# Last feed-forward of an eight-part transformer kernel: up products of four tiles issued together on disjoint rows of TensorE, each into its own bank

## What is computed

```python
unperm = jnp.argsort(perm)
t = x.reshape(b * l, Dm)[:, perm].reshape(b * l, h, d)      # 1024 tokens, 16 heads, 32
t = jnp.einsum('bhd,hdm->bhm', t, up)                       # 32 -> 128 for each head
t = jax.nn.gelu(t, approximate=False)
t = jnp.einsum('bhm,hmd->bhd', t, down)                     # 128 -> 32 for each head
out = t.reshape(b * l, h * d)[:, unperm]
```

## Time and profile before

| | us |
|---|---|
| median of 3 runs | 1510.85 (1509.21 to 1513.04) |
| the profiled execution, its own time | 1513.07 |
| its span in the trace | 1511.1 |
| PE busy / DVE / ACT / POOL | 1366.1 / 966.1 / 595.7 / 529.4 |
| mean granted clock of PE, share of full speed | 0.951 |

### The profile page before, as it was taken

One profiled execution on the slowest core, in us unless ns is written; L12 is line 12 of the kernel. 1 busy time (PEld: TensorE's weight loads), 2 busy tenths in 40 slices (PEclk: granted clock), 3 DMA queues, 4 the chain that ended last, 5 costly groups with the idle time before them and its releaser, 6 DMA issues.

```text
span 1511.1 us, 20683 instructions
## 1 busy us (share of the span) xinstructions
PE 1366.1 (90%) x6966; PEld 1020.6 (68%) x6966; DVE 966.1 (64%) x2126; ACT 595.7 (39%) x1605; POOL 529.4 (35%) x531
## 2 busy tenths in 40 slices
PE   2888877888998999989999889999999999998798
PEld 1555544666677777667877677777777787776555
DVE  6999956587432688832222666777777777776633
ACT  2777762361222345432212224444344443443331
POOL 5001003532222444132211354454454544543163
PEclk9999976998997999989999999999999999999799
DMA  5211112312121000011110231111211111100001
GB/s 163 57 43 30 33 32 91 104 63 82 44 77 49 1 15 29 1 42 43 42 42 15 91 105 35 49 36 50 64 56 49 36 49 63 57 22 1 7 1 56
DMA packets 54251, 72.76 MB, mean 48 GB/s; under 512 B 6130, under 2 KB 24818, under 8 KB 54148
## 3 DMA queue, kind: packets, MB, share of 16 engines
q1 hardware_dynamic: 53168, 70.20, 14.8%
q10 hardware_dynamic: 980, 1.25, 0.2%
HBM read 56.75 MB, written 10.49 MB: 44 GB/s over the span
## 4 chain that ended last, share of the span: by engine, by line
PE 65%; DVE 18%; issue 6%; POOL 5%; ACT 3%; DMA 2%; SPq 1%; POOLq 0%; DVEq 0%; ACTq 0%
PE bank L412 16%; PE bank L417 14%; PE bank L416 14%; PE bank L2318 3%; PE bank L2296 2%; PE bank L2211 2%; PE bank L2193 2%; DVE topv L1534 2%; DVE xn L1804 1%; DVE top L1528 1%; PE bank L2305 1%; PE bank L479 1%; DVE bank L1826 1%; DVE xn L1790 1%; DMA ring_l<-k 1%
## 5 line engine op out<-in xcount | busy, mean ns | idle before, releaser
L1005 POOL TENSOR_TENSOR ring_l<-stage,ring_h 128x512 fp32r<-128x512 f32 x133 | 179.0, 1364 | 236.4 <-ACT ring_h L1162 236.4
L412 PE MATMUL bank<-xTh_b,ring_h 128*128 128x512 f32 x464 | 191.0, 412 | 2.9 <-issue 1.5
L416 PE MATMUL bank<-xTl_b,ring_h 128*128 128x512 f32 x464 | 185.1, 399 | 0.0
L417 PE MATMUL bank<-xTh_b,ring_l 128*128 128x512 f32 x464 | 184.9, 399 | 0.0
L1113 POOL TENSOR_TENSOR q<-xn 128x512 f32<-128x512 f32 x64 | 82.3, 1285 | 221.0 <-DVE xn L1804 221.0
L412 PE MATMUL bank<-ring_h,o3h 128*128 128x512 f32 x256 | 125.5, 490 | 0.8 <-issue 0.8
L1444 ACT ACTIVATE probsT<-bank 128x512 f32<-128x512 f32 x64 | 38.3, 599 | 205.5 <-PE bank L2305 205.5
L1453 ACT ACTIVATE probs<-bank,nbias 128x128 f32<-128x128 f32 x256 | 90.7, 366 | 54.3 <-DVE nbias L1828 54.3
L412 PEld LDWEIGHTS bank<-xTh_b,ring_h 128*128 128x128 f32 x464 | 88.6, 191 | 23.3 <-issue 4.5
L417 PEld LDWEIGHTS bank<-xTh_b,ring_l 128*128 128x128 f32 x464 | 88.2, 190 | 21.7
L416 PEld LDWEIGHTS bank<-xTl_b,ring_h 128*128 128x128 f32 x464 | 88.7, 191 | 18.6
(11 more groups left out here) (323 smaller groups left out, 3324.9 us busy)
## 6 DMA issues: line engine op xcount, KB each, us to landing
stage<-in_units_dram SPq DMA_DIRECT2D x133, 256.0 KB, 3.1
ring_l<-k SPq DMA_DIRECT2D x64, 64.0 KB, 2.1
raw_k<-kvs SPq DMA_DIRECT2D x16, 256.0 KB, 2.1
raw_v<-kvs SPq DMA_DIRECT2D x16, 256.0 KB, 2.0
kraw<-raw_k SPq DMA_DIRECT2D x16, 256.0 KB, 3.4
v<-raw_v SPq DMA_DIRECT2D x16, 256.0 KB, 2.9
stage<-in_context_dram SPq DMA_DIRECT2D x8, 256.0 KB, 2.9
mask<-in_mask_row_dram SPq DMA_DIRECT2D x8, 256.0 KB, 3.1
```

The costliest lines, as they stand in the source:

```text
L412: ins = nc.tensor.matmul(out_ap, wh, mh, start=start, stop=False)
L416: nc.tensor.matmul(out_ap, wh, ml, start=False, stop=False)
L417: return nc.tensor.matmul(out_ap, wl, mh, start=False, stop=stop)
L1005: nc.gpsimd.tensor_tensor(ring_l[:, place_of(u), :], stage[:, u % STAGE, :], f32(ring_h[:, place_of(u), :]), ALU.subtract).then_inc(w_lo, 1)
```

## The change

The up products of a group's four heads are issued as one block of twelve matmuls (`four_up`): high by high of heads 0 to 3, then high by low of the four, then low by high. Each head has its own 32 rows of PE's array and its own bank, 0 to 3; the block raises `z_up` once, at its end. It waits for all four gelus of the group before. The permuted products move to banks 4 and 5, and from the third on each waits for the low half of the one two before. PE's new order is permuted(0), permuted(1), block 0, permuted(2), and then for each group o: down products 4o and 4o + 1, block o + 1, down products 4o + 2 and 4o + 3, permuted(o + 3). `tile_hi(o + 3)` and `tile_lo(o + 3)` now stand behind gelu and cast 4o + 3. `gel` has three places in place of two. `t2h` and `t2l` are laid over `tTh` and `tTl`, as permuted products still read `xTh_b` when the first sums of a group are copied away. The matmuls, gelus, casts and subtractions are the same in number and size.

```diff
--- before.py
+++ after.py
@@ -358,7 +358,7 @@
         e4.close()
         eB.close()
 
-        t2h, t2l = xTh_b, xTl_b
+        t2h, t2l = tTh, tTl
 
         kbh = xTh_b[:, 0:2, :].rearrange("r a (h j) -> r a h j", h=8)
         kbl = xTh_b[:, 2:4, :].rearrange("r a (h j) -> r a h j", h=8)
@@ -1150,7 +1150,7 @@
                 g.wait_ge(z_gh, n + 1)
                 if n >= 2:
                     g.wait_ge(z_dp, n - 1)
-                nc.gpsimd.tensor_tensor(gel_l[:, n % 2, :], gel[:, n % 2, :], f32(gel_h[:, n % 2, :]), ALU.subtract).then_inc(z_gl, 1)
+                nc.gpsimd.tensor_tensor(gel_l[:, n % 2, :], gel[:, n % 3, :], f32(gel_h[:, n % 2, :]), ALU.subtract).then_inc(z_gl, 1)
 
 
         @block.scalar
@@ -1468,7 +1468,7 @@
             def tile_hi(n):
                 a.wait_ge(z_t, n + 1)
                 c = slice(n % 2 * HALF, (n % 2 + 1) * HALF)
-                nc.scalar.activation(tTh[:, n // 2, c], bank[n % 4][:], ACT.Copy).then_inc(z_th, 1)
+                nc.scalar.activation(tTh[:, n // 2, c], bank[4 + n % 2][:], ACT.Copy).then_inc(z_th, 1)
 
             for n in range(3):
                 tile_hi(n)
@@ -1479,12 +1479,12 @@
                 nc.scalar.activation(t2h[:, o // 2, c], bank[6 + o % 2][:], ACT.Copy).then_inc(z_oh, 1)
 
             for n in range(32):
-                a.wait_ge(z_up, n + 1)
-                if n >= 2:
-                    a.wait_ge(z_gl, n - 1)
-                nc.scalar.activation(gel[:, n % 2, :], bank[4 + n % 2][:], ACT.Gelu).then_inc(z_g, 1)
-                if n < 5:
-                    tile_hi(n + 3)
+                a.wait_ge(z_up, n // 4 + 1)
+                if n >= 3:
+                    a.wait_ge(z_gl, n - 2)
+                nc.scalar.activation(gel[:, n % 3, :], bank[n % 4][:], ACT.Gelu).then_inc(z_g, 1)
+                if n % 4 == 3 and n // 4 + 3 < 8:
+                    tile_hi(n // 4 + 3)
                 if n % 4 == 2 and n > 4:
                     last_hi(n // 4 - 1)
             last_hi(7)
@@ -1852,7 +1852,7 @@
             def tile_lo(n):
                 v.wait_ge(z_th, n + 1)
                 c = slice(n % 2 * HALF, (n % 2 + 1) * HALF)
-                nc.vector.tensor_tensor(tTl[:, n // 2, c], bank[n % 4][:], f32(tTh[:, n // 2, c]), ALU.subtract).then_inc(z_tl, 1)
+                nc.vector.tensor_tensor(tTl[:, n // 2, c], bank[4 + n % 2][:], f32(tTh[:, n // 2, c]), ALU.subtract).then_inc(z_tl, 1)
 
             for n in range(3):
                 tile_lo(n)
@@ -1878,9 +1878,9 @@
                 v.wait_ge(z_g, n + 1)
                 if n >= 2:
                     v.wait_ge(z_dp, n - 1)
-                nc.vector.tensor_copy(gel_h[:, n % 2, :], gel[:, n % 2, :]).then_inc(z_gh, 1)
-                if n < 5:
-                    tile_lo(n + 3)
+                nc.vector.tensor_copy(gel_h[:, n % 2, :], gel[:, n % 3, :]).then_inc(z_gh, 1)
+                if n % 4 == 3 and n // 4 + 3 < 8:
+                    tile_lo(n // 4 + 3)
                 if n % 4 == 3 and n > 4:
                     last_lo(n // 4 - 1)
             last_lo(7)
@@ -2335,44 +2335,58 @@
             t.wait_ge(ln_lo, B * (LN_L3F[1] + 1))
             def permuted(n):
 
-                if n >= 4:
-                    t.wait_ge(z_tl, n - 3)
+                if n >= 2:
+                    t.wait_ge(z_tl, n - 1)
                 c = slice(n % 2 * HALF, (n % 2 + 1) * HALF)
                 for k in range(KT):
                     if n == 0:
                         t.wait_ge(z_pick, k + 1)
                     w = pick[:, k, n // 2 * P:(n // 2 + 1) * P]
-                    nc.tensor.matmul(bank[n % 4][:], w, xTh_b[:, k, c], start=k == 0, stop=False)
-                    ins = nc.tensor.matmul(bank[n % 4][:], w, xTl_b[:, k, c], start=False, stop=k == KT - 1)
+                    nc.tensor.matmul(bank[4 + n % 2][:], w, xTh_b[:, k, c], start=k == 0, stop=False)
+                    ins = nc.tensor.matmul(bank[4 + n % 2][:], w, xTl_b[:, k, c], start=False, stop=k == KT - 1)
                 ins.then_inc(z_t, 1)
 
-            for n in range(3):
-                permuted(n)
             uh, ul = unit(U_L3F)
-            for n in range(34):
-                if n < 32:
-                    i4, half, gr = n // 8, n // 4 % 2, slice(32 * (n % 4), 32 * (n % 4) + 32)
-                    if n % 4 == 0:
-                        t.wait_ge(z_tl, n // 4 + 1)
-                    if n >= 2:
-                        t.wait_ge(z_g, n - 1)
-                    w, c = slice(i4 * P, (i4 + 1) * P), slice(half * HALF, (half + 1) * HALF)
-                    mm3(bank[4 + n % 2][:], uh[gr, w], ul[gr, w], tTh[gr, i4, c], tTl[gr, i4, c], True, True).then_inc(z_up, 1)
-                    if n < 5:
-                        permuted(n + 3)
-                m = n - 2
-                if m >= 0:
-                    o = m // 4
-                    if m == 0:
-                        t.wait_ge(z_dn, 1)
-                    if m % 4 == 0 and o >= 2:
-                        t.wait_ge(z_ol, o - 1)
-                    t.wait_ge(z_gl, m + 1)
-                    hh = 4 * (m // 8) + m % 4
-                    dst = bank[6 + o % 2][:]
-                    nc.tensor.matmul(dst, down_h[:, hh, :], gel_h[:, m % 2, :], start=m % 4 == 0, stop=False)
-                    nc.tensor.matmul(dst, down_l[:, hh, :], gel_h[:, m % 2, :], start=False, stop=False)
-                    nc.tensor.matmul(dst, down_h[:, hh, :], gel_l[:, m % 2, :], start=False, stop=m % 4 == 3).then_inc(z_dp, 1)
+
+            def four_up(o):
+
+                t.wait_ge(z_tl, o + 1)
+                if o:
+                    t.wait_ge(z_g, 4 * o)
+                w, c = slice(o // 2 * P, (o // 2 + 1) * P), slice(o % 2 * HALF, (o % 2 + 1) * HALF)
+                for part in range(3):
+                    for q in range(4):
+                        gr = slice(32 * q, 32 * q + 32)
+                        ins = nc.tensor.matmul(bank[q][:], (uh, uh, ul)[part][gr, w], (tTh, tTl, tTh)[part][gr, o // 2, c],
+                                               start=part == 0, stop=part == 2)
+                ins.then_inc(z_up, 1)
+
+            def one_down(m):
+
+                o, hh = m // 4, 4 * (m // 8) + m % 4
+                if m == 0:
+                    t.wait_ge(z_dn, 1)
+                if m % 4 == 0 and o >= 2:
+                    t.wait_ge(z_ol, o - 1)
+                t.wait_ge(z_gl, m + 1)
+                dst = bank[6 + o % 2][:]
+                nc.tensor.matmul(dst, down_h[:, hh, :], gel_h[:, m % 2, :], start=m % 4 == 0, stop=False)
+                nc.tensor.matmul(dst, down_l[:, hh, :], gel_h[:, m % 2, :], start=False, stop=False)
+                nc.tensor.matmul(dst, down_h[:, hh, :], gel_l[:, m % 2, :], start=False, stop=m % 4 == 3).then_inc(z_dp, 1)
+
+            permuted(0)
+            permuted(1)
+            four_up(0)
+            permuted(2)
+            for o in range(8):
+                one_down(4 * o)
+                one_down(4 * o + 1)
+                if o + 1 < 8:
+                    four_up(o + 1)
+                one_down(4 * o + 2)
+                one_down(4 * o + 3)
+                if o + 3 < 8:
+                    permuted(o + 3)
             t.wait_ge(z_pick, KT + 1)
             t.wait_ge(z_ol, 8)
             for b in range(B):
```

## The result

The changed kernel takes 1535.75 us (median of four, 1534.09 to 1538.84) against 1510.84 us before (median of four): ratio 1.0166, 95% interval 1.0144 to 1.0189, so 25 us slower. The profiled execution took 1534.09 us, with a span of 1531.9 us.

What follows compares the result with a forecast made beforehand. PE was taken to bound the kernel (1.77 us a round), the cast and subtraction loop close behind (1.65 floor). 18.9 - 0.5 + 1.9 + 11.5 = +31.8 us on 1513.1 gives 1544.9, brought to the median 1543 us; range 1526 to 1558.

Steps and rivals of the forecast that it cites:

- the five groups: Last stage, groups with an uncovered permuted product: 57.6 us against 38.7 for their 20 casts, +18.9 us.
- the last twelve tiles: Groups six to eight, up to the first put product: 23.4 us against 23.9, -0.5 us.
- the start: Start of the last stage: block 0 ahead of permuted(2) moves DVE's work before the first cast, +1.9 us.
- the put stage: After the last tiles: no term; a change in its time (18 us) was named as a sign of a wrong forecast.
- The term of the clock: Groups one to six: clock falls in PE's idle, 2.0 us each for two to six, 1.5 for the first, +11.5.
- "clock holds" rival: In PE's idle in the groups the clock does not fall, so 11.5 us go: 1531 us, 18 in 100.
- The block: Twelve up products, 0.11 us apart: 2.0 us from last product before to first after, against 3.6; PE saves 1.6.
- A group at full clock: In the five groups, first cast to the next group's first cast: 11.65 us, or 11.0 for the first group.
- the second cast: In each of the five groups, it slips in ahead of the first subtraction: +0.35 us, bound 0 to 0.4.
- the fourth subtraction: In each of the five groups, the third and fourth subtraction lie beside the up block, adding no term.
- Serial up products: In the blocks, up products 0.23 us apart, each of seven blocks 1.4 us longer: 1553 us, 16 in 100.
- The faster case: In the groups, permuted product stays hidden and the 1.65 us cast and subtraction loop binds: 1508.5 us, 3 in 100.

Runs made afterwards that it cites:

- the fillers: The changed kernel with PE's idle filled by products whose result nobody reads (also called the filler kernel): 1530.44 us, ratio 1.0111.
- shared subtractions: Changed kernel, copies of permuted(3) to (7) three tiles later, DVE taking three of four subtractions, four places for gel_h and gel_l: 1504.39 us, ratio 0.9945.
- the kernel before with shared subtractions: The kernel before, without the block, DVE taking three of four subtractions, four places for gel_h and gel_l: 1516.95 us, ratio 1.0032.

## Why the prediction was right, and where it was off

The forecast was 1543 us, slower, by a chain in five groups; it came out at 1536, inside the range, which was 32 us wide. By the ledger, with the clock's term spread over the groups that it was put to, the five groups were forecast at +28.4 us and measured +20.65, the last twelve tiles +1.5 and -0.4, the start +1.9 and +1.45, the put stage 0 and +1.5: 31.8 against 23.2.

- *The mechanism.* The permuted product, its copies in front of gelu 4o+4, and PE's idle of 3.3 us in the first of five groups and 3.9 in the others are in the trace as forecast, and moving only the copies took all 25 us back. One sign that was named as speaking against the forecast did appear: the time of the put stage changed, from 17.9 to 19.5 us. It came from the same clock and not from another mechanism, as the fillers brought it back to 18.0. Group distances of 11.75 to 12.0 us lie between my 11.65 (full clock) and 13.7 (low clock).
- *The term of the clock, 11.5 us,* was the mis-sized one: the fillers give 8 in the medians and 6.9 in the traces. Of the 6.9, 1.6 us lie in the put stage, where I had put nothing; in the six groups and the tiles behind them it is 5.0 where I had 11.5. The clock was low for 3.4 us in each of the second to fifth groups, less than the two down trios, the block and part of the next two trios that I took: in the third it was back at 1458.3, as the block began. The "clock holds" rival, 1531 us, is not what happened, but it was nearly the filler kernel's 1530.
- *The block.* I took 1.65 us from its first product to the next down product, by the distance of two weight loads. It is 0.93 us: the loads overlap as well, the lower bound of the step. The Trainium skill (TensorE: Matmul & The Clock Gate, Measured speedup vs the span model) has a speedup of 3.07 for four row tiles of 512 columns, which gives an estimate of 0.9 us for twelve products of 2.8 us in all; by that rule, the trace agrees with 2.99 against 0.93, a factor of 3.2.
- *A group at full clock,* 11.65 us, measures 11.24 in the filler kernel. The block is 0.7 us shorter, and the second cast cost almost nothing where I had +0.35: the first two subtractions run in 2.6 us. Against that, with a shorter block the fourth subtraction came on the path, which I had taken as covered: PE waits 0.50 us for it at 1460.56, and 0.62 us in the filler kernel.
- *The five groups* 18.9 us at full clock: the filler kernel has 1431.35 to 1486.94 = 55.6 us against 38.7, +16.9. *The last twelve tiles* -0.5, measured -0.4; that they agree is luck, as the full-clock number meant here is the filler kernel's 22.2 us against 23.9, -1.7, and 1.3 us of low clock hide it. *The start* +1.9, measured +1.45, as the block is shorter.
- *The rivals.* Serial up products: excluded by 0.93 against 2.99. The faster case did need what I named, PE reaching the permuted product without ACT's gelus behind it; with the copies moved it still gave only a draw, 0.9996. The 32 tiles did get 3.7 us shorter, near the 4.2 that 1.78 against 1.65 us a tile gave, though not evenly: groups with two low halves stay at 7.1 us. What I had wrong there was the rest, 1.1 us at the start and 1.6 in the put stage, which I had at 1.9 and nothing.

Left open: why one idle or another of about 4 us leaves the clock down for 3.4 us or 6.8, and why it fell behind a busy PE in two of the experiments, was not tried. Nor was it tried whether ACT's copy or DVE's had to move, what holds a group at 6.75 us with shared subtractions, or whether the block's wait for four gelus costs anything once both other bounds are gone.

## What to carry to other kernels

Before an engine is relieved, compute what the next loop allows: here PE took 1.78 us a tile and DVE with POOL 1.65 at best, so a PE gain of 1.6 us a block (2.3 in the filler kernel) could bring at most 0.13 us a tile, 4 us in all, until the subtractions were shared. And where an operand's preparation is moved in one engine's list, move its copies in the others' lists by need, not by symmetry: a wait for work that is not needed until two groups later, put ahead of work that is ready, cost 25 us together with the clock that fell in the idle, and moving the two copies back returned it.

## What the runs showed of the hardware

- Products on disjoint 32-row groups start within some hundredths of a microsecond of each other, weight loads included, whatever their order in the program (four first products at 1460.77, the first head's second at 1461.37): PE lets one row group's product overtake another's. Twelve took 0.93 us, on the same rows 2.99.
- The exclusion of DVE and POOL is not only of casts and subtractions: building a 0/1 matrix on DVE took 4.93 us in place of 1.67 beside two clearings of 2.08 us on POOL.
- The granted clock fell in a stretch where PE was busy for 91% of the time with 32-row products on one row group among full ones (mean 0.84), and held at 0.99 where it was busy for 82% with the products of four row groups side by side. In the kernel before with shared subtractions it fell at 1490.75, after 50 us in which PE was busy for 99% and one idle of 0.85 us; the kernel before, with an idle of 0.81 us at the same place, kept it. The runs don't say why.
